# Denominators straight behind the product with V in all twelve key tiles, row-maximum pieces at three places a tile, and zero rows written between the x tiles

## The chip, the cores and the metric

The kernel runs on one core of one Trainium2 chip. The metric is the device time of one execution of the whole kernel in microseconds (us), the median of three runs. Its engines are TensorE (PE in the rows: matmuls; PEld: its weight loads), VectorE (DVE), ScalarE (ACT), GpSimd (POOL) and SyncE (SP, which here only issues transfers). Each works through its own list of instructions in order; they wait for each other by semaphores.

## The reference, cut to what matters

Four layers work on x of 2 x 1024 x 1024: attention, a mixing layer, a second attention and a layer with a small mixture of experts. Only the two attentions are touched. Both have 32 query heads, 8 key heads and a head size of 32, so that four query heads share one key head:

```python
q = (x @ wq).reshape(bsz, seq_len, N_HEADS, HEAD_DIM)
k = (x @ wk).reshape(bsz, seq_len, N_KV_HEADS, HEAD_DIM)
v = (x @ wv).reshape(bsz, seq_len, N_KV_HEADS, HEAD_DIM)
...
scores = jnp.einsum('bqhd,bkhd->bhqk', q, k) / np.float32(np.sqrt(HEAD_DIM))
scores = scores + mask
attn = jax.nn.softmax(scores.astype(jnp.float32), axis=-1).astype(q.dtype)
out = jnp.einsum('bhqk,bkhd->bqhd', attn, v).reshape(bsz, seq_len, N_HEADS * HEAD_DIM)
return out @ wo
```

## The kernel before, in words

**Groups.** `attention` is called once for each of the two attentions. For each of the two batches it runs a prologue (projections, first row maxima) and then eight groups, one per key head with its four query heads. Groups 0 to 5 of a batch follow the order `body`, group 6 `body6` (without a projection), group 7 `body7`, or `ahead7` in the first batch, which also prepares the next batch's x. That makes 24 groups of `body`, 4 of `body6`, 2 of `body7` and 2 of `ahead7` in the kernel.

**Tiles and steps.** A group has twelve key tiles (units 0 to 11): pairs of 512 queries and 128 keys on or below the diagonal. The list that `iteration` returns sets the order of every engine's work in the group. Its steps are:

- `("ST", e, half)`: scores of unit e, transposed, for two of the four heads (two matmuls into `pst`, line 827). ScalarE takes the exponential into `prob` (line 560), GpSimd masks a unit on the diagonal (line 464).
- `("PV", e, 0)`: the product of `prob` with V (`vg`) into `ppv`, below called V e. `("PV", e, 1)`: the product of the same `prob` with a matrix of ones into `pden`, the softmax denominators, below D e. Each is four products of 32 output rows, line 847, shown as x8 in the trace.
- `("S", k)`: piece k of the row maxima of the next group, k from 0 to 37. TensorE writes untransposed scores of one to four heads, at most 512 columns, into one of the two banks of `psh` (line 780). VectorE takes the maximum: line 650 for a piece below the diagonal, line 647 with its read of the accumulator for a piece on the diagonal, once per head.
- `("P", c, i)`: an eighth of a projection of 512 columns, three matmuls of line 759, also into `psh`. `MT`, `NORM`, `HI`, `LO`, `WS`, `RS` and others are steps of the other engines, or short.

**The two banks.** `bank_plan` gives pieces and projections the banks 0 and 1 of `psh` in turn. A piece may start when VectorE has freed its bank, that is when it has read the piece two before:

```python
pe.wait_ge(s["sh_free"], SH0 + u + prev + 1)
```

This wait stands ahead of the piece's weight load. Everything behind it in TensorE's list waits too.

**Where the pieces stand.** `iteration` spreads the 38 pieces over all steps of units 1 to 9 (`window`), in proportion to the columns that each step streams. `after[step]` holds what follows a step.

**The start of an attention.** For eight x tiles VectorE takes statistics and normalises (line 619), GpSimd computes 1/deviation (line 420), and TensorE transposes. GpSimd then writes the constant rows of `kst` and `qst` (lines 492, 494, 496), turns the first projection (`turn_over`, lines 432 and 434), and splits the second chunk of weights (`w_lo`, line 425), for which TensorE's second chunk of projections waits. The semaphore `padded` tells TensorE that the constant rows stand; it is read ahead of the first piece.

Of the kernel before, what the change touches and what calls it, by code (L numbers as in the profile page):

```python
# [14 lines left out]
F32 = mybir.dt.float32  # L15
# [6 lines left out]
P = 128  # L22
# [3 lines left out]
ST_ = S // P  # L26
# [3 lines left out]
GH = 4  # L30
# [46 lines left out]
def columns(step):  # L77

    what, e, _ = step
    n = BANK - unit_offset(e)  # L80
    return 2 * max(n, BANK // 2) if what == "ST" else 4 * n


def iteration(full_s=True, proj=True, ahead=False):

    steps = [[("ST", e + 1, 0), ("ST", e + 1, 1), ("PV", e, 0), ("PV", e, 1)] for e in range(NU)]
    steps[-1] = steps[-1][2:]  # L90
    after = {step: [] for unit in steps for step in unit}
    first = []
    if proj:
        quarter = lambda c, i: [("P", c, k) for k in range(i * PIECES // 4, (i + 1) * PIECES // 4)]
        first = quarter(0, 0)
        for i, step in enumerate(steps[0][:3]):
            after[step] += quarter(0, i + 1)
        after[steps[2][1]] += [("HI", 0)]
        after[steps[3][1]] += [("LO", 0)]
        after[steps[2][0]] += [("WL", 0)]  # L100
        after[steps[4][0]] += [("WS", 0)]
        after[steps[5][0]] += [("RS", 0)]
        after[steps[10][1]] += quarter(1, 0)
        after[steps[10][2]] += quarter(1, 1) + [("RK", 0)]
        after[steps[10][3]] += quarter(1, 2) + quarter(1, 3)
    if full_s:
        window = [step for unit in steps[1:10] for step in unit]
        total, done, k = sum(map(columns, window)), 0, 0
        for step in window:
            done += columns(step)  # L110
            while k < len(USES) and k * total < done * len(USES) - total // 2:
                after[step] += [("S", k)]
                k += 1
        assert k == len(USES)
        after[steps[10][1]] += [("MT", 0)]
    after[steps[10][1]] += [("NORM", 0)]
    if ahead:


        for i in range(ST_):  # L120
            after[steps[i][0]] += [("XS", i)]
            after[steps[i][2]] += [("XN", i)]
            after[steps[i + 2][1]] += [("XT", i)]
            after[steps[i + 2][2]] += [("XC", i)] + [("XL", i + NX_AHEAD)] * (i + NX_AHEAD < ST_)
        first = [("XL", i) for i in range(NX_AHEAD)]
        for i in range(PIECES):
            after[steps[10][i * 3 // PIECES]] += [("P", "next", i)]
    order = [("ST", 0, 0), ("ST", 0, 1)] + ([("HI", 1), ("LO", 1), ("RS", 1)] if full_s else []) + first
    for unit in steps:
        for step in unit:  # L130
            order += [step] + after[step]
    return order + [("NORM", 1)]


# [55 lines left out]
def attention(nc, sem, layer, x_in, wqkv, cos_in, sin_in, swap, oT_d):  # L190
# [21 lines left out]
    ZT0, W0, SH0, R0, E0, PV0, AC0, N0, ST0, DMA0 = 4, 2, 1, 4, 2, 2, 2, 1, 2, 16  # L212

    pro, body, body6, body7 = prologue(), iteration(), iteration(proj=False), iteration(False, False)
    ahead7 = iteration(False, False, True)
    plan_pro, U_PRO = bank_plan(pro, spare=(2, 3, 4, 5))
    plan = {id(order): bank_plan(order)[0] for order in (body, body6, body7, ahead7)}
# [4 lines left out]
    with ExitStack() as ctx:  # L222
        def sb(name, shape, dt=F32):
            return ctx.enter_context(nc.sbuf_tensor(f"a{layer}_{name}", shape, dt))
# [17 lines left out]
        qst = [sb(f"qst{i}", [P, GH, S], F32R) for i in range(2)]  # L242
# [173 lines left out]
        def _(pool):  # L416
            def reciprocal_deviation(tile, k):

                pool.wait_ge(s["stats"], tile + 1)
                pool.tensor_tensor(mv[k % 2][:, 3:4], mv[k % 2][:, 2:3], nhalf[:, :], ALU.pow).then_inc(s["pow"], 1)  # L420

            def w_lo(n, par):
                pool.wait_ge(s["w_hi"], n + 1)
                pool.sem_inc(s["pool_turn"], 1)
                pool.tensor_tensor(w[par][1][:, :, :], wraw[par][:, :, :], w[par][0][:, :, :].bitcast(F32),  # L425
                                   ALU.subtract).then_inc(s["w_ready"], 1)
# [56 lines left out]
            pool.drain().then_inc(s["const"], 1)  # L483
            pool.drain().then_inc(s["w_ready"], W0)
            pool.drain().then_inc(s["roped"], R0)
            for k in range(ST_):
                reciprocal_deviation(k, k)
                if k == 5:
                    w_lo(0, 0)
            pool.drain()  # L490
            for i in range(2):
                pool.memset(kst[i][96:P, :].bitcast(F32), -1.0)
                pool.drain()
                pool.memset(kst[i][96:P - 1, :].bitcast(F32), 0.0)
                pool.drain()
                pool.memset(qst[i][96:P - 1, :, :].bitcast(F32), 0.0)
                pool.drain()
            pool.drain().then_inc(s["padded"], 1)

# [248 lines left out]
        def _(pe):  # L748
            def project(n, u, where, par, c, piece):

                _, at, prev = where
                if piece == 0:
                    pe.wait_ge(s["w_ready"], W0 + n + 1)
                    pe.wait_ge(s["sh_free"], SH0 + u + prev + 1)
                passes = [(k, a, x) for k in range(KC) for a, x in ((0, 0), (0, 1), (1, 0))]
                step = len(passes) // PIECES
                for i in range(piece * step, (piece + 1) * step):
                    k, a, x = passes[i]
                    mm = pe.matmul(bank(at), w[par][a][:, k, :], xT[x][:, k, c * BANK:(c + 1) * BANK],  # L759
                                   start=(i == 0), stop=(i == len(passes) - 1))  # L760
                if piece == PIECES - 1:
                    mm.then_inc(s["sh_ready"], 1)
# [12 lines left out]
            def row_scores(u, where, par, k):  # L775
                _, at, prev = where
                qt, kc, n, heads, _ = USES[k]
                pe.wait_ge(s["sh_free"], SH0 + u + prev + 1)
                for i, h in enumerate(heads):
                    mm = pe.matmul(psh[:, at, i * n:(i + 1) * n], qst[par][0:P - 1, h, qt * P:(qt + 1) * P],  # L780
                                   kst[par][0:P - 1, kc * BANK:kc * BANK + n], start=True, stop=True,
                                   skip_group_check=True)
                mm.then_inc(s["sh_ready"], 1)

            def transpose_max(n, u, where):
                _, at, prev = where
                pe.wait_ge(s["mx_ready"], n + 1)
                pe.wait_ge(s["sh_free"], SH0 + u + prev + 1)
                pe.transpose(psh[0:GH * ST_, at, 0:P], mx[:, 0, :], ident[:, :]).then_inc(s["sh_ready"], 1)
# [1131 lines left out]
```

## Time and profile before

| | before |
|---|---|
| median of three runs | 3116.89 us (3111.95 to 3116.89) |
| the profiled execution's own time | 3121.41 us |
| its span, from the first to the last instruction | 3119.7 us |
| mean granted TensorE clock over the span | 0.945 |
| TensorE busy (matmuls) | 2780.3 us, 89% |
| VectorE busy | 1933.4 us, 62% |
| ScalarE busy | 1001.4 us, 32% |
| GpSimd busy | 715.2 us, 23% |

The span is the time that the rows below divide up. The profiled execution's own time is 1.7 us longer, and lies 4.5 us above the median of the three runs. A share of busy time is an average over all layers. What one stage waits for is read from that stage's rows.

### The profile page before, as it was taken

Reading aid. Unit: us, or ns where it says so; the run is one execution under the profiler, and the core shown is the slowest. Engines: PE = TensorE matmul, PEld = TensorE weight load, DVE = VectorE, ACT = ScalarE, POOL = GpSimd, SP = SyncE. Lnnn points to the kernel's source line nnn. Section 1 sums busy time; section 2 is a strip of 40 time slices with the busy share of each in tenths; the row PEclk is TensorE's granted clock in tenths of the full one; section 3 lists DMA queues with packets and bytes.
Section 4 is the critical chain, followed back from the end, with each engine's and each line's share of the span. In section 5 each row is a group of like instructions: output and inputs, shape, how many; then the busy total and the mean of one; then the engine's idle time right before and its main releaser. Section 6 shows DMA issues by size and latency. Waiting matters only on the chain. (4 is left out here: it accounts for less than half of the span.)

```text
span 3119.7 us, 49191 instructions
## 1 busy us (share of the span) xinstructions
PE 2780.3 (89%) x15824; PEld 1788.4 (57%) x15824; DVE 1933.4 (62%) x4357; ACT 1001.4 (32%) x1549; POOL 715.2 (23%) x693
## 2 busy tenths in 40 slices
PE   7899998999999799652859999989999996997999
PEld 5545554655554488652646455436555542885887
DVE  4577777557777433588765677775677774324543
ACT  2143435134343411352521443433244344101000
POOL 6223231433231000000044323214223220001111
PEclk8999999999999899765979999989999998998999
DMA  3323222323131422000123323223323221443111
GB/s 139 102 64 89 70 72 72 113 73 97 56 102 30 140 81 67 0 0 0 81 115 105 101 63 89 69 64 110 94 63 97 58 77 73 158 135 148 68 67 41
DMA packets 121063, 252.84 MB, mean 81 GB/s; under 512 B 12720, under 2 KB 39728, under 8 KB 120880
## 3 DMA queue, kind: packets, MB, share of 16 engines
q1 hardware_dynamic: 120912, 251.03, 25.5%
q8 instruction: 69, 1.13, 0.2%
q14 instruction: 82, 0.67, 0.1%
HBM read 166.57 MB, written 84.41 MB: 80 GB/s over the span
## 5 line engine op out<-in xcount | busy, mean ns | idle before, releaser
L560 ACT ACTIVATE a_prob<-a_pst 128x1024 f32<-128x1024 f32 (+3 forms) x768 | 593.0, 814 | 726.2 <-PE a_pst L827 724.7
L647 DVE CUSTOM_DVE_ANT_0 a_psh<-a_psh,a_edge 128x128 f32<-128x128 f32 (+3 forms) x1024 | 487.6, 514 | 218.5 <-PE a_psh L780 208.1
L780 PE MATMUL a_psh<-a_kst,a_qst 127*128 127x512 f32 (+3 forms) x1536 | 511.7, 394 | 29.3 <-issue 12.0
L780 PEld LDWEIGHTS a_psh<-a_kst,a_qst 127*128 127x128 f32 x1536 | 255.9, 189 | 455.4 <-DVE a_mx L647 199.3
L827 PE MATMUL a_pst<-a_qst,a_kst 128*128 128x512 f32 (+2 forms) x1536 | 398.8, 361 | 28.9 <-ACT a_prob L560 11.0
L650 DVE TENSOR_REDUCE a_mx<-a_psh 128x1 f32<-128x512 f32 x512 | 343.6, 689 | 71.1 <-PE a_psh L780 65.1
L847 PE MATMUL a_ppv<-a_prob,a_vg 128*32 128x512 f32 (+3 forms) x3072 | 335.0, 508 | 15.6 <-POOL a_prob L464 10.6
L464 POOL TENSOR_SCALAR_AFFINE_SELECT a_prob<-a_prob 128x512 f32<-128x512 f32 x256 | 171.9, 672 | 759.4 <-ACT a_prob L560 758.2
L827 PEld LDWEIGHTS a_pst<-a_qst,a_kst 128*128 128x128 f32 x1536 | 267.1, 192 | 128.4 <-issue 56.2
L847 PE MATMUL a_pden<-a_prob,a_ones 128*32 128x512 f32 (+3 forms) x3072 | 332.0, 504 | 0.0
L691 DVE RECIPROCAL a_dens<-a_dens 128x512 f32<-128x512 f32 x64 | 214.6, 3353 | 75.6 <-ACT a_dens L568 66.4
L432 POOL TENSOR_TENSOR a_swp<-a_swp,a_sin 128x512 f32<-128x512 f32 x80 | 103.2, 1290 | 330.3 <-DVE a_swp L636 329.6
L759 PE MATMUL a_psh<-a_xT_hi,a_w_hi 128*128 128x512 f32 x416 | 174.4, 419 | 2.3 <-issue 1.6
L1411 PE MATMUL h_pout<-h_w,h_o 128*128 128x512 f32 x720 | 167.7, 392 | 0.8 <-DVE h_x L1288 0.8
L759 PE MATMUL a_psh<-a_xT_lo,a_w_hi 128*128 128x512 f32 x416 | 165.2, 397 | 0.0
L759 PE MATMUL a_psh<-a_xT_hi,a_w_lo 128*128 128x512 f32 x416 | 164.9, 396 | 0.0
L425 POOL TENSOR_TENSOR a_w_lo<-a_wraw,a_w_hi 128x1024 fp32r<-128x1024 f32 x50 | 119.2, 2383 | 178.9 <-ACT a_w_hi L536 163.0
L759 PE MATMUL a_pst<-a_xT_hi,a_w_hi 128*128 128x512 f32 x352 | 141.7, 403 | 13.2 <-POOL a_w_lo L425 9.0
L1411 PEld LDWEIGHTS h_pout<-h_w,h_o 128*128 128x128 f32 x720 | 134.1, 188 | 28.8 <-DMA h_wb<-in_w_branch 1.2
L647 DVE DVE_READ_ACCUMULATOR2_ANT a_mx<- 128x1 f32 x1024 | 145.0, 142 | 0.0
L759 PE MATMUL a_pst<-a_xT_lo,a_w_hi 128*128 128x512 f32 x352 | 139.5, 396 | 0.0
L759 PE MATMUL a_pst<-a_xT_hi,a_w_lo 128*128 128x512 f32 x352 | 139.1, 395 | 0.0
(217 smaller groups left out, 3958.8 us busy)
## 6 DMA issues: line engine op xcount, KB each, us to landing
a_qst<-q SPq DMA_DIRECT2D x192, 256.0 KB, 4.5
a_wraw<-in_wqkv SPq DMA_DIRECT2D x52, 512.0 KB, 5.7
q<-a_stg_hi SPq DMA_DIRECT2D x64, 256.0 KB, 2.6
q<-a_stg_lo SPq DMA_DIRECT2D x64, 256.0 KB, 2.8
oT<-a_oT SPq DMA_DIRECT2D x64, 256.0 KB, 2.5
a_kst<-kT SPq DMA_DIRECT2D x96, 128.0 KB, 3.0
h_oraw<-oT SPq DMA_DIRECT2D x16, 512.0 KB, 4.1
h_x<-in_x SPq DMA_DIRECT2D x16, 512.0 KB, 4.7
```

The source lines that it names most:

```text
L425: pool.tensor_tensor(w[par][1][:, :, :], wraw[par][:, :, :], w[par][0][:, :, :].bitcast(F32), ALU.subtract).then_inc(s["w_ready"], 1)
L432: pool.tensor_tensor(swp[c][:, :], swp[c][:, :], sin[:, c * BANK:(c + 1) * BANK], ALU.mult)
L464: pool.affine_select(out=blk, in_=blk, compare_op=ALU.is_ge, fill=0.0, base=0, pattern=[[0, GH], [1, P]], channel_multiplier=-1)\
L560: act.activation(prob[k % 2][:, 2 * half:2 * half + 2, off:], pst[:, half, :, off:], ACT.Exp, scale=scale).then_inc(s["exp_done"], 1)
L647: part = dve.tensor_tensor_reduce(scores, scores, edge[:, BANK - n:], 1.0, 2 * MASKED, ALU.add, ALU.max, mx_hq[kc][:, h, qt:qt + 1])
L650: part = dve.tensor_reduce(mx_hq[kc][:, heads[0]:heads[0] + m, qt], psh[:, at, 0:m * n].rearrange("p (m n) -> p m n", n=n), AX.X, ALU.max)
L691: dve.reciprocal(dens[:, :], dens[:, :])
L759: mm = pe.matmul(bank(at), w[par][a][:, k, :], xT[x][:, k, c * BANK:(c + 1) * BANK], start=(i == 0), stop=(i == len(passes) - 1))
L780: mm = pe.matmul(psh[:, at, i * n:(i + 1) * n], qst[par][0:P - 1, h, qt * P:(qt + 1) * P], kst[par][0:P - 1, kc * BANK:kc * BANK + n], sta ...
L827: mm = pe.matmul(pst[:, half, hh, off:], kst[par][:, ki * P:(ki + 1) * P], qst[par][:, 2 * half + hh, qc * BANK + off:(qc + 1) * BANK], st ...
L847: mm = pe.matmul(acc[h * HD:(h + 1) * HD, off:], lhs, prob[k % 2][:, h, off:], start=(ki == 0), stop=(ki == 4 * qc + 3), skip_group_check= ...
L1411: mm = pe.matmul(pout[:, half, :], o[:, par, a, k, :], w[:, b, k, half * BANK:(half + 1) * BANK], start=(i == 0), stop=(i == len(passes) - 1))
```

## The change

`open_slots` keeps the two ST steps and D of each unit as places behind which pieces are put, and takes out V. What stood behind V is now put behind D, ahead of what stood there already. So D follows V directly in all twelve units, and the pieces have three places a unit: behind each of the two ST steps and behind D. At the start of each attention the constant rows of `kst` are written first, and the zero rows of `qst` in eight parts (one head of one of the two buffers), each behind the 1/deviation of one x tile.

```diff
+def open_slots(units):
+
+    return [step for unit in units for step in unit if step[0] != "PV" or step[2] == 1]
...
     if full_s:
-        window = [step for unit in steps[1:10] for step in unit]
+        window = open_slots(steps[1:10])
...
     for unit in steps:
         for step in unit:
-            order += [step] + after[step]
+            if step[0] == "PV" and step[2] == 0:
+                order += [step]
+            elif step[0] == "PV":
+                order += [step] + after["PV", step[1], 0] + after[step]
+            else:
+                order += [step] + after[step]
...
-            for k in range(ST_):
-                reciprocal_deviation(k, k)
-                if k == 5:
-                    w_lo(0, 0)
-            pool.drain()
             for i in range(2):
                 pool.memset(kst[i][96:P, :].bitcast(F32), -1.0)
                 pool.drain()
                 pool.memset(kst[i][96:P - 1, :].bitcast(F32), 0.0)
                 pool.drain()
-                pool.memset(qst[i][96:P - 1, :, :].bitcast(F32), 0.0)
+            for k in range(ST_):
+                reciprocal_deviation(k, k)
+                if k == 5:
+                    w_lo(0, 0)
+                pool.drain()
+                pool.memset(qst[k // GH][96:P - 1, k % GH, :].bitcast(F32), 0.0)
                 pool.drain()
             pool.drain().then_inc(s["padded"], 1)
```

The first place is TensorE's list in `body`, around the products of unit 5. Before, from the second ST of unit 6 (which stands ahead of V 5) to piece 18; `a_pst` is ST, `a_ppv` is V, `a_pden` is D, `a_psh` with `a_kst` is a piece:

```order
L827 MATMUL a_pst<-a_qst,a_kst 128x512 x2
L778 REGISTER_ALU
L780 MATMUL a_psh<-a_kst,a_qst 128x128 x4
L841 REGISTER_ALU
L847 MATMUL a_ppv<-a_prob,a_vg 32x512 x4
L778 REGISTER_ALU
L780 MATMUL a_psh<-a_kst,a_qst 128x512
L847 MATMUL a_pden<-a_prob,a_ones 32x512 x4
L778 REGISTER_ALU
L780 MATMUL a_psh<-a_kst,a_qst 128x512
L778 REGISTER_ALU
L780 MATMUL a_psh<-a_kst,a_qst 128x512
```

And now, at the same place (line numbers are ten higher):

```order
L837 MATMUL a_pst<-a_qst,a_kst 128x512 x2
L788 REGISTER_ALU
L790 MATMUL a_psh<-a_kst,a_qst 128x512
L851 REGISTER_ALU
L857 MATMUL a_ppv<-a_prob,a_vg 32x512 x4
L857 MATMUL a_pden<-a_prob,a_ones 32x512 x4
L788 REGISTER_ALU
L790 MATMUL a_psh<-a_kst,a_qst 128x512
L788 REGISTER_ALU
L790 MATMUL a_psh<-a_kst,a_qst 128x512
L788 REGISTER_ALU
L790 MATMUL a_psh<-a_kst,a_qst 128x512
```

Piece 16, which parted V 5 from D 5, now stands ahead of V 5, and three pieces (17, 18, 19) instead of two stand behind D 5 before the next ST.

The second place is GpSimd's list at the start of an attention, from the end of its constants to the first `turn_over`. Before (`a_mv` is the 1/deviation of an x tile, `a_swp` the first instruction of `turn_over`):

```order
L420 TENSOR_TENSOR a_mv<-a_mv,a_nhalf 128x1 x6
L425 TENSOR_TENSOR a_w_lo<-a_wraw,a_w_hi 128x1024
L420 TENSOR_TENSOR a_mv<-a_mv,a_nhalf 128x1 x2
L492 MEMSET a_kst 32x1024
L494 MEMSET a_kst 31x1024
L496 MEMSET a_qst 31x4096
L492 MEMSET a_kst 32x1024
L494 MEMSET a_kst 31x1024
L496 MEMSET a_qst 31x4096
L432 TENSOR_TENSOR a_swp<-a_swp,a_sin 128x512
```

And now its last part, from the sixth x tile on (the four `a_kst` rows and five pairs like the first two rows stand ahead):

```order
L430 TENSOR_TENSOR a_mv<-a_mv,a_nhalf 128x1
L435 TENSOR_TENSOR a_w_lo<-a_wraw,a_w_hi 128x1024
L506 MEMSET a_qst 31x1024
L430 TENSOR_TENSOR a_mv<-a_mv,a_nhalf 128x1
L506 MEMSET a_qst 31x1024
L430 TENSOR_TENSOR a_mv<-a_mv,a_nhalf 128x1
L506 MEMSET a_qst 31x1024
L442 TENSOR_TENSOR a_swp<-a_swp,a_sin 128x512
```

Only one short memset is left between the last 1/deviation and `turn_over`. VectorE's, ScalarE's, SyncE's and GpSimd's order in the groups stays as it was, but for `ahead7`, where ScalarE copies the accumulators of unit 3 ahead of an x tile. The bank of every piece stays the same too.

## Rows read from the trace of the kernel before

**Rows 1.** The page: granted TensorE clock in 40 slices, tenths of full speed.

```profile
PEclk8999999999999899765979999989999998998999
```

**Rows 2.** Four `body` groups: busy time by engine; longest waits among weight loads.

```profile
242.40:454.29 211.89, 211.40 (x1349) 111.37 (x1349) 157.89 (x369) 88.81 (x124) 63.05 (x64) 1.00 0.27 78
...
PEld a_psh L780 <- DVE a_mx L647: 24.4, 40, 0.8
...
PEld a_psh L780 <- DVE a_mx L650: 21.1, 32, 0.8
```

**Rows 3.** Timeline of PE: start, us, engine, line, operation; first rows of two groups.

```profile
911.15 1.21 PE L827 MATMUL a_pst<-a_qst,a_kst 128*128 128x512 f32 x4
...
964.14 1.21 PE L827 MATMUL a_pst<-a_qst,a_kst 128*128 128x512 f32 x4
```

**Rows 4.** Timeline of PE in `body`: piece 16 to piece 20.

```profile
936.54 0.51 PE L780 MATMUL a_psh<-a_kst,a_qst 127*128 127x512 f32 x1
936.98 1.06 PE L847 MATMUL a_pden<-a_prob,a_ones 128*32 128x512 f32 x8
937.97 0.73 PE L780 MATMUL a_psh<-a_kst,a_qst 127*128 127x512 f32 x2
938.54 0.64 PE L827 MATMUL a_pst<-a_qst,a_kst 128*128 128x512 f32 x2
939.26 0.50 PE L780 MATMUL a_psh<-a_kst,a_qst 127*128 127x512 f32 x1
939.59 0.63 PE L827 MATMUL a_pst<-a_qst,a_kst 128*128 128x512 f32 x2
940.07 0.40 PE L780 MATMUL a_psh<-a_kst,a_qst 127*128 127x256 f32 x2
```

**Rows 5.** Timeline of DVE: maxima of piece 8 and of pieces 17 to 19.

```profile
929.41 0.70 DVE L647 CUSTOM_DVE_ANT_0 a_psh<-a_psh,a_edge 128x512 f32<-128x512 f32 x1 [0.25 <-PE a_psh L780]
930.02 0.14 DVE L647 DVE_READ_ACCUMULATOR2_ANT a_mx<- 128x1 f32 x1
...
938.51 1.98 DVE L650 TENSOR_REDUCE a_mx<-a_psh 128x1 f32<-128x512 f32 x3 [0.73 <-PE a_psh L780]
```

**Rows 6.** Timeline of PE in `body7`, where nothing parts V and D.

```profile
1034.22 1.06 PE L847 MATMUL a_ppv<-a_prob,a_vg 128*32 128x512 f32 x8
1035.10 1.04 PE L847 MATMUL a_pden<-a_prob,a_ones 128*32 128x512 f32 x8
1036.07 1.20 PE L827 MATMUL a_pst<-a_qst,a_kst 128*128 128x512 f32 x4
```

**Rows 7.** Timeline of POOL at the start of the first attention.

```profile
29.64 0.95 POOL L492 MEMSET a_kst<- 32x1024 f32 x1
...
41.81 1.28 POOL L432 TENSOR_TENSOR a_swp<-a_swp,a_sin 128x512 f32<-128x512 f32 x1 [0.37 <-issue]
...
44.46 2.34 POOL L425 TENSOR_TENSOR a_w_lo<-a_wraw,a_w_hi 128x1024 fp32r<-128x1024 f32 x1
```

**Rows 8.** Timeline of DVE at the start of the first attention.

```profile
24.66 0.81 DVE L619 TENSOR_SCALAR a_prob<-a_prob,a_mv 128x1024 f32<-128x1024 f32 x1
...
30.56 1.65 DVE L619 TENSOR_SCALAR a_xin<-a_xin,a_mv 128x1024 f32<-128x1024 f32 x1
...
36.23 0.72 DVE L711 STREAM_SHUFFLE a_swp<-a_psh 128x512 f32<-128x512 f32 x1
```

**Rows 9.** Timeline of PE at the start of both attentions.

```profile
46.85 0.80 PE L759 MATMUL a_pst<-a_xT_hi,a_w_hi 128*128 128x512 f32 x1 [4.06 <-POOL a_w_lo L425]
...
50.37 0.40 PE L759 MATMUL a_pst<-a_xT_hi,a_w_lo 128*128 128x512 f32 x1
50.60 0.39 PE L759 MATMUL a_pst<-a_xT_hi,a_w_hi 128*128 128x512 f32 x1
...
1632.51 0.80 PE L759 MATMUL a_pst<-a_xT_hi,a_w_hi 128*128 128x512 f32 x1 [4.92 <-POOL a_w_lo L425]
...
1637.37 0.46 PE L759 MATMUL a_pst<-a_xT_hi,a_w_lo 128*128 128x512 f32 x1
```

## The prediction, made before the changed kernel ran

> **What bounds the kernel now.** I read the page first: TensorE's busy share is the highest of the engines (the table above), and the granted clock stands near full speed in most slices [rows 1]. The share over the whole kernel says little, so I went on to the stage that the change touches. In four `body` groups (211.89 us) TensorE is busy for 211.40 us and the clock is granted in full [rows 2]. So a `body` group is bound by TensorE's list: whatever its matmuls take, or wait for, is the time. One group lasts 964.14 - 911.15 = 53.0 us [rows 3].
>
> The same view has a warning. TensorE's weight loads for the pieces wait for VectorE in 40 + 32 = 72 of the 4 x 38 = 152 pieces, 45.5 us in all [rows 2]. These waits cost almost nothing today because the matmuls ahead of the piece are still streaming. They show that the two banks are handed back only just in time.
>
> **What the edit of the order saves.** The change lets D follow V without a piece between. I read the price of parting them from the timeline of TensorE. D 5 takes 937.97 - 936.98 = 0.99 us until the next matmul, which is a piece [rows 4]; V followed by D takes 1035.10 - 1034.22 = 0.88 us [rows 6]. Leaving a product for another kind of matmul costs 0.11 us. The single 512-column piece between V and D takes 936.98 - 936.54 = 0.44 us [rows 4], where the same matmul among its like takes 0.23 us (50.60 - 50.37 in a projection [rows 9]; two ST matmuls of 512 columns take 940.07 - 939.59 = 0.48 us [rows 4]). So 0.21 us go to being first behind a product and last ahead of one. Together a split costs 0.32 us; I take 0.31, since some splits hold smaller pieces.
>
> In `body` V and D are parted in ten units (0, 1, 2, 4 to 10), in `body6` in eight (1, 2, 4 to 9), in `ahead7` in one, in `body7` in none. That is 3.1, 2.5, 0.3 and 0 us a group.
>
> **What it adds.** All pieces now stand at three places, and V and D together are a block of about 1.9 us (0.88 + 0.99) in which VectorE can have at most the two pieces that the two banks hold. Behind the block come up to three pieces in a row. The third needs the bank of the first.
>
> The turnaround of a bank is in the rows. Pieces 17 and 18 start at 937.97; VectorE starts on 17 at 938.51, 0.54 later; three maxima in a row take 1.98 us, which is 0.69 for one and 0.645 for each further; piece 19, in the bank of 17, starts at 939.26, so 1.29 us behind 17 [rows 4, 5]. It followed an ST step that began at 938.54 and needed 0.46, so it was some 0.26 us late, and its slot was 939.59 - 939.26 = 0.33 us, not 0.23: a late piece also shows its weight load.
>
> Now put three 512-column pieces directly behind D. The third could start at 0.34 + 0.23 = 0.57 us and gets its bank at 1.29: 0.72 us of wait. That is the case for pieces 17, 18, 19; for 22, 23, 24; and for 32, 33, 34. A maximum on the diagonal is slower: its read of the accumulator comes 0.61 us after its start and takes 0.14, and the bank is free only then [rows 5].
>
> I walked through a whole `body` group in this way, TensorE's list against VectorE's: a matmul of 512 columns 0.23, 384 0.18, 256 0.12 and 128 0.10 us, a product by 4/2400 us a column, the 0.11 and 0.2 us of each change of kind, 0.54 us from a piece to its maximum where VectorE is free, 0.645 us for a maximum below the diagonal, 0.06 from a free bank to the piece. For the order of before the walk gives 53.1 us a group against the 53.0 measured, with 0.6 us of waits for banks (at piece 19 above all, as in [rows 4]). For the new order it gives these waits: piece 3 0.84, piece 4 0.25, 8 0.37, 11 0.50, 14 0.27, 15 0.31, 19 0.73, 24 0.73, 27 0.32, 30 0.53, 34 0.73, and 0.49 at the projection step behind piece 37. The sum is 6.1 us, 5.5 more than before. Eleven late starts instead of six show their weight load, 0.1 us each: 0.5 more. Against that stand the 3.1 us of the splits. Net +2.9 us for `body`.
>
> `body6` has the same pieces and eight splits: 6.0 - 2.5 = +3.5; I take 3.4, since its last wait overlaps with one that it has for the row maxima. `ahead7` gains 0.3. The sum is 24 x 2.9 + 4 x 3.4 - 2 x 0.3 = 69.6 + 13.6 - 0.6 = **+82.6 us**.
>
> What is queued behind the waiting piece is the next ST or V. ScalarE and GpSimd get their scores later, but they idle between units today; the next group's row maxima come later by what the group grows and are still needed only at its end. They add nothing.
>
> **The zero rows.** At the start of an attention TensorE waits 4.06 us for `w_lo`, from 42.79 on; in the second attention 4.92 us [rows 9]. `w_lo` ran at 44.46, behind `turn_over` at 41.81, behind six memsets from 29.64 to 0.37 us before `turn_over` [rows 7]. VectorE had the projection ready at 36.95 [rows 8]. Without the memsets `turn_over` starts at 37.05, takes 2.65, `w_lo` 2.34: ready at 42.04, ahead of TensorE. The wait goes. The idle time had a second price: behind it TensorE runs at half clock, eight matmuls in 50.37 - 46.85 = 3.52 us where 0.23 each make 1.8, and in the second attention eleven in 4.86 where they need 2.5 [rows 9]. So 4.06 + 1.7 + 4.92 + 2.3 = 13.0 us are gained.
>
> The memsets now lie where VectorE works, and there is one price. A normalisation takes 0.81 us, and 1.65 with a memset on GpSimd at its side [rows 7, 8]: it waited. Today one of eight does. In the new order the four `kst` memsets (1.07 each) end near 7 us, when the first 1/deviation is due, and the first `qst` part may catch the first normalisation; later a part ends over 1 us before the next. So one is paid and one saved, about zero; if none is saved, 2 x 0.85 = 1.7 are lost. If the clock would have dropped anyway, only 9.0 are gained. Bounds -7 to -13; I take **-13**.
>
> **Sum.** +82.6 - 13.0 = +69.6 us on the profiled execution, 3121.4 to 3191. That execution lay 4.5 us over the median, which gives **3187 us**.
>
> **Unknown costs.** The walk rests on hand-over times. With the hand-over 0.07 us shorter, banks handed back at once, or maxima of 0.60 us, a `body` group gains 2.6 to 2.8 us. If a late piece hides its weight load, 2.4. If the 0.1 us for the first matmul behind a product is not saved by joining, 3.6. I widen to 2.0 and 3.7: 28 groups make +56 to +104, with the zero rows +43 to +97.
>
> **The rivals.**
>
> 1. *The banks keep up, and the splits' price is simply saved* (faster). V and D joined save 24 x 3.1 + 4 x 2.5 + 0.6 = 85 us, and the zero rows 13: 3117 - 98 = 3019 us. For it speaks that VectorE is idle for a quarter of a group (157.89 of 211.89 busy [rows 2]). Against it, the 1.29 us turnaround is seen in the rows and lies against 0.57 us of work. It decides if the waits grow by less than 3.1 us a group; my walk says 6.0. Chance 0.06.
>
> 2. *The waits grow by about what the joins save* (near zero or slightly faster). With some 3 us a group only the 13 us are left, and 3104 us follow; with 3.6 us, no change. Its mechanism is VectorE starting on a piece earlier than its row shows. Chance 0.06.
>
> 3. *The clock falls too* (slower still). TensorE would sit idle twelve times a group. At the start of the attentions it ran at half clock after an idle stretch, and lost 1.7 us in each fall that short [rows 9]. One such fall in each of 28 groups adds 48 us: 3235 us. Against it, the four groups show full clock [rows 2] and no single new wait is over 0.9 us. The Trainium skill, TensorE: Matmul & The Clock Gate, section on the second failure mode (cycling through PSUM banks), says that short idles between groups of matmuls, forced by the queue of banks, can swing the clock; it speaks against this change, and the trace so far shows such a fall only behind idle times of over 4 us. Chance 0.08.
>
> My forecast has 0.80.
>
> **Range and chances.** The forecast's own range of +43 to +97 is 3160 to 3214. To hold 8 in 10 I let it reach part of the way to the clock case above and to smaller waits below: 3150 to 3222. From here 0.2% is 6 us, about what a measurement of this kernel can tell from no change. Faster by more: rival 1 and most of 2, 0.10. Within: 0.02. Slower: 0.88.
>
> **What the profile of the changed kernel would show.** Right: a `body` group of 55.9 us, V and D of 512 columns 0.88 us apart, the third piece behind D 1.3 us behind the first, TensorE's idle time before line 790 by VectorE at some 6 us a group; no wait for `w_lo` at the start of the attentions and full clock there; normalisations of 0.81 us but for at most one. Wrong: groups of 50 us (rival 1), or below 1.0 granted clock in the groups (rival 3). I would be wrong too if the walk misses a coupling that the old order never used, such as ScalarE's exponential coming too late for V.

## The result, and the profile after

The changed kernel takes 3182.86 us (median of 4 runs, 3178.94 to 3187.77) against 3116.89 us (median of 4 runs, 3111.95 to 3120.95): a ratio of 1.0212, 95% interval 1.0199 to 1.0225, so 66 us slower. The forecast was 3187 us. The profiled execution took 3178.94 us with a span of 3177.2 us; its span is 57.5 us longer than that of before. Its mean clock is 0.949.

The page of the changed kernel: span, busy times, the granted clock in 40 slices, and from its list of costliest groups the pieces (busy time, mean ns of one, and behind the bar the idle time of TensorE just before them):

```profile
span 3177.2 us, 49229 instructions
PE 2741.3 (86%) x15824; PEld 1813.0 (57%) x15824; DVE 1912.5 (60%) x4357; ACT 1009.9 (32%) x1549; POOL 714.0 (22%) x705
PEclk9999999999999899866979999999999999998999
L790 PE MATMUL a_psh<-a_kst,a_qst 127*128 127x512 f32 (+3 forms) x1536 | 511.3, 389 | 121.0 <-DVE a_mx L660 46.3
```

TensorE is busy for 39 us less (89% to 86% of the span) and the kernel is longer: work was saved and waiting put in its place. 121.0 us of idle time stand directly before pieces; before the change they were 29.3 us.

Four `body` groups of the changed kernel by windows (span of the stretch, then busy time of PE, PEld, DVE, ACT and POOL, clock, DMA share, GB/s), and what TensorE's matmuls waited for in them (total us, times, longest us):

```profile
1853.06:2074.89 221.83, 206.66 (x1352) 115.75 (x1348) 154.39 (x369) 90.09 (x124) 62.95 (x64) 1.00 0.27 74
...
PE a_psh L790 <- DVE a_mx L660: 6.6, 12, 0.6
PE a_psh L790 <- DVE a_mx L657: 5.2, 12, 0.6
PE a_psh L769 <- DVE a_mx L657: 1.1, 4, 0.3
```

Before, TensorE was busy for 211.40 of 211.89 us here [rows 2]. Now it is for 206.66 of 221.83: a group has 15.17 / 4 = 3.8 us of idle time. The clock stays at 1.00, and VectorE has not more to do than before; it has only its work at other times. A whole group by its first rows (as [rows 3]), and the place of [rows 4], where three pieces stand behind a product:

```profile
936.87 1.21 PE L837 MATMUL a_pst<-a_qst,a_kst 128*128 128x512 f32 x4
...
963.01 1.07 PE L857 MATMUL a_ppv<-a_prob,a_vg 128*32 128x512 f32 x8
963.89 1.04 PE L857 MATMUL a_pden<-a_prob,a_ones 128*32 128x512 f32 x8
964.86 0.73 PE L790 MATMUL a_psh<-a_kst,a_qst 127*128 127x512 f32 x2
966.15 0.50 PE L790 MATMUL a_psh<-a_kst,a_qst 127*128 127x512 f32 x1 [0.55 <-DVE a_mx L660]
966.48 0.62 PE L837 MATMUL a_pst<-a_qst,a_kst 128*128 128x512 f32 x2
...
992.47 1.21 PE L837 MATMUL a_pst<-a_qst,a_kst 128*128 128x512 f32 x4
```

One group takes 992.47 - 936.87 = 55.60 us; over the 20 `body` groups that are not the first of a batch the mean is 55.49, against 53.02 (in the four groups of the windows 55.46 against 52.97). V to D is 963.89 - 963.01 = 0.88 us, as in [rows 6], and D to the next matmul 0.97. The third piece behind D starts 966.15 - 964.86 = 1.29 us behind the first and takes 966.48 - 966.15 = 0.33 us. VectorE's timeline shows the other side of that wait:

```profile
965.40 1.98 DVE L660 TENSOR_REDUCE a_mx<-a_psh 128x1 f32<-128x512 f32 x3 [1.23 <-PE a_psh L790]
```

VectorE had waited 1.23 us for this piece, since no piece comes during V and D. It starts 0.54 us behind the piece (965.40 - 964.86), and needs 0.69 us for the maximum; then the bank is free. TensorE and VectorE now wait for each other in turn.

The start of the first attention after the change: GpSimd, VectorE and TensorE.

```profile
7.73 0.95 POOL L506 MEMSET a_qst<- 31x1024 f32 x1
...
25.39 0.95 POOL L506 MEMSET a_qst<- 31x1024 f32 x1
...
37.60 1.30 POOL L442 TENSOR_TENSOR a_swp<-a_swp,a_sin 128x512 f32<-128x512 f32 x1 [5.60 <-DVE a_swp L721]
...
40.29 2.40 POOL L435 TENSOR_TENSOR a_w_lo<-a_wraw,a_w_hi 128x1024 fp32r<-128x1024 f32 x1
```

```profile
7.73 1.50 DVE L629 TENSOR_SCALAR a_xin<-a_xin,a_mv 128x1024 f32<-128x1024 f32 x1
...
25.34 1.55 DVE L629 TENSOR_SCALAR a_prob<-a_prob,a_mv 128x1024 f32<-128x1024 f32 x1
...
31.62 0.93 DVE L629 TENSOR_SCALAR a_xin<-a_xin,a_mv 128x1024 f32<-128x1024 f32 x1
...
36.71 0.72 DVE L721 STREAM_SHUFFLE a_swp<-a_psh 128x512 f32<-128x512 f32 x1
```

```profile
42.66 0.39 PE L769 MATMUL a_pst<-a_xT_lo,a_w_hi 128*128 128x512 f32 x1
42.89 0.39 PE L769 MATMUL a_pst<-a_xT_hi,a_w_lo 128*128 128x512 f32 x1
43.12 0.39 PE L769 MATMUL a_pst<-a_xT_hi,a_w_hi 128*128 128x512 f32 x1
```

`turn_over` starts at 37.60 instead of 41.81 [rows 7], `w_lo` is ready at 42.69, and TensorE's second chunk follows with 0.23 us a matmul and no wait, where [rows 9] had 4.06 us of wait and half clock behind it. The first memset and the first normalisation run side by side at 7.73, and the normalisation takes 1.50 us for 0.81. The same happens once more, at the sixth x tile: there the memset stands behind a `w_lo`, starts at 25.39, and the normalisation beside it takes 1.55 us. The last one, which took 1.65 [rows 8], takes 0.93. So two are stretched, where before it was one.

### The profile page after: what moved, and what is told of

Read it like the earlier page. It is cut to its first block and busy times, and to the rows that moved or that the text cites. A ratio compares the mean times of both kernels' runs of the same rounds, so it can differ in the third digit from the quotient of the medians.

```text
span 3177.2 us, 49229 instructions
## 1 busy us (share of the span) xinstructions
PE 2741.3 (86%) x15824; PEld 1813.0 (57%) x15824; DVE 1912.5 (60%) x4357; ACT 1009.9 (32%) x1549; POOL 714.0 (22%) x705
## 5 line engine op out<-in xcount | busy, mean ns | idle before, releaser
L790 PE MATMUL a_psh<-a_kst,a_qst 127*128 127x512 f32 (+3 forms) x1536 | 511.3, 389 | 121.0 <-DVE a_mx L660 46.3
L837 PE MATMUL a_pst<-a_qst,a_kst 128*128 128x512 f32 (+2 forms) x1536 | 411.8, 363 | 28.1 <-DMA a_qst<-rowmax 10.2
L857 PE MATMUL a_pden<-a_prob,a_ones 128*32 128x512 f32 (+3 forms) x3072 | 323.5, 493 | 0.0
L857 PEld LDWEIGHTS a_pden<-a_prob,a_ones 128*32 128x32 f32 x3072 | 100.3, 112 | 155.7 <-issue 144.9
```

Of the source, the lines that this page charges most:

```text
L837: mm = pe.matmul(pst[:, half, hh, off:], kst[par][:, ki * P:(ki + 1) * P], qst[par][:, 2 * half + hh, qc * BANK + off:(qc + 1) * BANK], st ...
L857: mm = pe.matmul(acc[h * HD:(h + 1) * HD, off:], lhs, prob[k % 2][:, h, off:], start=(ki == 0), stop=(ki == 4 * qc + 3), skip_group_check= ...
```

## The experiments

The kernel before ran beside the experiments, on the chip that they ran on. Its median was 3116.94 us beside the first four, and 3114.59 us beside the last four. Ratios are against it. The `body` group of a table is the mean of four or more groups of the run's trace.

### The two parts apart

`e1_zero_rows_only` is the kernel before with only the new place of the memsets. `e2_order_only` is the changed kernel with the memsets where they were.

> The kernel before with only the zero rows moved between the x tiles. Theory A (the wait for w_lo and the half clock behind it go): TensorE starts its second chunk of projections without a wait in both attentions, and the kernel gains 4.7 us before the first group and some 7 us in the second attention, 12 us in all, about 3105 us beside 3117. Rival B (a memset at the side of a normalisation delays the x tiles and eats the gain): under 6 us. Rival C (the gain is given back at the first pieces, which wait for their keys and queries by DMA): the first group starts earlier but its third unit no earlier, under 3 us in all.

> The changed kernel with the zero rows written as before, so the new order alone. Theory A (two parts that add up): a body group of 55.5 us as in the changed kernel, 53.0 before, and 66 + 12 = 78 us over the kernel before, about 3195 us. Rival (part of the slowdown came from the earlier start, such as the first group's longer waits for its keys and queries): 66 us over the kernel before or less, about 3183 us.

| | median us | runs | ratio (95% interval) | span | `body` group |
|---|---|---|---|---|---|
| `e1_zero_rows_only` | 3104.54 | 7 | 0.9961 (0.9947 to 0.9975) | 3101.7 | 52.9 to 53.0 |
| `e2_order_only` | 3195.96 | 4 | 1.0253 (1.0233 to 1.0273) | 3190.9 | 55.45 |

The memsets alone give -12.4 us (3104.54 - 3116.94), the order alone +79.0. Together they make +66.6, and both at once were measured at +66.0. So the two parts add up within 1 us, and the slower kernel hides a gain of 0.4%.

### V and D joined in one unit alone

Here the kernel before keeps its order, but for one unit of the 24 `body` groups: in `e3_join_10` D follows V directly in unit 10, in `e4_join_0` in unit 0. What stood behind V goes behind D.

```diff
+JOINED = (10,)
...
-            order += [step] + after[step]
+            if step[0] == "PV" and step[1] in JOINED and full_s and proj:
+                order += [step] + (after["PV", step[1], 0] + after[step] if step[2] else [])
+            else:
+                order += [step] + after[step]
```

> The kernel before, with D straight behind V in unit 10 of body alone; projection steps, no row-maximum pieces, stood between. Theory A (a split costs 0.31 us where no bank is short): 24 x 0.31 = 7.4 us faster, about 3109 us, a body group of 52.7 us. Rival (the price of a split is no price of TensorE's time, because what follows waits for the banks anyway): no change, 3117 us.

> The same edit in unit 0 of body alone, where the last two steps of the first projection stood between. Theory A (bound by the two banks): the projection now ends just ahead of piece 0, VectorE turns it (1.35 us) when the first pieces want their banks, and piece 1 or 3 waits; my walk through the two lists gives 53.8 us a body group, 0.9 us more, so about 20 us slower, 3138 us. Rival B (only the split counts): 7.4 us faster, 3109 us.

| | median us | runs | ratio (95% interval) | span | `body` group |
|---|---|---|---|---|---|
| `e3_join_10` | 3111.49 | 10 | 0.9978 (0.9965 to 0.9990) | 3112.5 | 52.6 |
| `e4_join_0` | 3133.29 | 7 | 1.0049 (1.0035 to 1.0062) | 3131.2 | 53.7 |

Joining is worth what the rows said when nothing else goes wrong: 0.38 us a group in the trace, and 5.45 / 24 = 0.23 us by the medians (0.13 to 0.45 by the interval), around the predicted 0.31.

In unit 0 the same edit costs 0.7 us a group. I had expected that size (0.9), but from a wait for a bank. The trace names another. In the waits of TensorE in four groups, and in its timeline, V 2 waits for GpSimd's mask:

```profile
1832.00:2046.71 214.71, 210.27 (x1348) 112.07 (x1348) 156.92 (x369) 89.03 (x124) 62.86 (x64) 1.00 0.27 76
...
PE a_ppv L851 <- POOL a_prob L468: 3.9, 4, 1.0
...
1846.43 0.64 PE L851 MATMUL a_ppv<-a_prob,a_vg 128*32 128x256 f32 x8 [0.97 <-POOL a_prob L468]
```

GpSimd's timeline shows why the mask is late:

```profile
1843.09 1.27 POOL L436 TENSOR_TENSOR a_swp<-a_swp,a_sin 128x512 f32<-128x512 f32 x1 [4.13 <-DVE a_swp L640]
1844.51 1.28 POOL L438 TENSOR_TENSOR a_rot<-a_rot,a_swp 128x512 f32<-128x512 f32 x1
1845.74 1.23 POOL L468 TENSOR_SCALAR_AFFINE_SELECT a_prob<-a_prob 128x512 f32<-128x512 f32 x2
```

The projection steps that stood between V 0 and D 0 now end later, so `turn_over` starts later, and the mask of unit 2 is behind it in GpSimd's list. So this run showed nothing of the banks. It showed a second price that my prediction did not have: a delayed projection can reach V through GpSimd. In the changed kernel no wait of V for the mask is among the waits of four groups above. What hides it there can be read from `e6_short_maxima_new`, two experiments below, which has the same order: the wait at piece 3 shrinks from 0.64 to 0.37 us, and V 2 waits 0.34 us for the mask instead. From the first ST of unit 3 to V 2 TensorE takes 2.05 us there, against 2.18 in the changed kernel.

```profile
1798.09 0.64 PE L857 MATMUL a_ppv<-a_prob,a_vg 128*32 128x256 f32 x8 [0.34 <-POOL a_prob L474]
```

So in the changed kernel TensorE reaches V 2 late already, by its waits at pieces 3 and 4, and nearly all of these two waits would be taken over by the mask if the banks came back sooner.

### The third pieces put elsewhere

`e5_third_piece_later` is the changed kernel with pieces 19, 24 and 34, the third ones directly behind a D of 512 columns, each moved behind the next ST. All other pieces stay. `PLACES` gives for each piece its step among those of units 1 to 9.

```diff
+PLACES = [0, 3, 3, 4, 5, 7, 8, 9, 9, 12, 13, 13, 15, 15, 16, 16, 17, 19, 19, 20, 20, 21, 23, 23, 24, 24, 25, 25, 27, 27, 28, 29, 31, 31, 32, 33, 35, 35]
...
-        window = open_slots(steps[1:10])
...
+        window = [step for unit in steps[1:10] for step in unit]
+        for k, place in enumerate(PLACES):
+            after[window[place]] += [("S", k)]
```

> The changed kernel with pieces 19, 24 and 34, each the third behind D, moved behind the first ST step of the next unit. Theory A (VectorE has only two pieces to work on during V and D, so the time lost is VectorE's, and a piece moved back by one ST waits there instead): a body group of 55.4 us, 0.1 us less, some 3 us in all, about 3180 us. Rival B (as my prediction worded it: the third piece behind D holds TensorE up by 0.72 us, and without three in a row the wait is gone): 28 x 3 x 0.72 = 60 us faster than the changed kernel, about 3123 us.

It took 3175.05 us (4 runs), ratio 1.0199 (1.0180 to 1.0218). That is 60.5 us over the kernel before beside it, where the changed kernel lay 66.0 over; the two intervals overlap, so the medians alone hardly tell them apart. A group takes 55.12 us instead of 55.46 in the traces. Windows and waits of four groups, then the timeline of TensorE at a unit where the wait now comes later:

```profile
1849.37:2069.86 220.49, 209.34 (x1353) 116.19 (x1349) 153.72 (x369) 91.47 (x124) 63.05 (x64) 1.00 0.27 74
...
PE a_psh L786 <- DVE a_mx L653: 5.4, 14, 0.6
PE a_psh L786 <- DVE a_mx L656: 1.2, 4, 0.3
...
1887.48 0.62 PE L786 MATMUL a_psh<-a_kst,a_qst 127*128 127x384 f32 x2
1888.79 0.50 PE L786 MATMUL a_psh<-a_kst,a_qst 127*128 127x512 f32 x1 [0.33 <-DVE a_mx L653]
```

The three waits of 0.72 us did go, but most of their time was lost again further on: against the changed kernel, unit 5 is 1.05 us shorter and unit 6 0.10, unit 7 is 0.97 longer, unit 8 1.07 shorter, unit 9 0.92 longer (each moved piece takes its own slot along). Of 3 x 0.72 = 2.2 us only 0.33 us a group are gained. So a late third piece was where the wait showed, not what made it. At the V and D of unit 5 VectorE stood idle for 1.23 us, before the change for 0.73 [rows 5], and the pieces that it didn't take then are due in the next units. A place that relieves one piece loads the next.

### VectorE's maxima made short

If VectorE's pace through two banks is what TensorE waits for, shorter maxima must give the time back, and must give far less to the kernel before. Both kernels take each maximum over only the first 128 columns of a head's scores, so that the maxima of larger pieces are incomplete, and on the diagonal take the mask's last 128 columns for them. All matmuls, places and banks stay.

```diff
-                        scores = psh[:, at, i * n:(i + 1) * n]
+                        scores = psh[:, at, i * n:i * n + P]
...
-                                             psh[:, at, 0:m * n].rearrange("p (m n) -> p m n", n=n), AX.X, ALU.max)
+                                             psh[:, at, 0:m * P].rearrange("p (m n) -> p m n", n=P), AX.X, ALU.max)
```

> The changed kernel with maxima over the first 128 columns of each head's scores alone; the rest of the columns is left out of the maximum. VectorE frees a bank in some 0.25 us a head, not up to 0.65. Theory A (bank and VectorE hold the time): the waits between the pieces go, and a body group falls from 55.5 to 51.9 us; 1.7 us of waits are left, at the first pieces, which wait for VectorE to turn the projection. About 28 x 3.5 = 98 us faster than the changed kernel, 3085 us. Rival (TensorE is slowed by the new order itself): no change, 3183 us.

> The kernel before with the same short maxima; the same columns are left out. Theory A: a body group falls from 53.0 to 52.0 us only, about 28 us, 3089 us. Rival (shorter maxima help by as much in either order, since VectorE is what is short): 98 us faster as in the new order, 3019 us.

| | median us | runs | ratio (95% interval) | `body` group |
|---|---|---|---|---|
| `e6_short_maxima_new` (changed kernel) | 3058.4 | 2 | 0.9823 (0.9799 to 0.9847) | 51.7 |
| `e7_short_maxima_old` (kernel before) | 3060.63 | 2 | 0.9830 (0.9807 to 0.9853) | 51.73 |

Four groups of each, `e6_short_maxima_new` first with its waits:

```profile
1783.73:1990.50 206.77, 201.78 (x1348) 115.93 (x1348) 106.08 (x369) 90.09 (x124) 62.89 (x64) 1.00 0.28 79
...
PE a_psh L790 <- DVE a_mx L657: 1.5, 4, 0.4
PE a_ppv L857 <- POOL a_prob L474: 1.4, 4, 0.3
PE a_psh L790 <- DVE a_mx L660: 0.9, 6, 0.2
```

```profile
1784.23:1991.15 206.92, 206.92 (x1353) 111.65 (x1349) 106.64 (x369) 88.33 (x124) 62.95 (x64) 1.00 0.28 79
```

In the new order a group gets 3.8 us shorter and the waits for banks shrink from 12.9 to 2.4 us in four groups: VectorE's pace is what the new order waits for. Both rivals fell: the new order was not slow by itself, and the order of before gained 1.24 us a group, a third as much. That is still more than the 0.6 us of waits that the walk gave it. So [rows 2], with 211.40 of 211.89 us busy, hid over 1 us a group: a late piece shows its weight load and a longer slot, which is counted as busy.

Both medians are some 27 us lower than expected (3085 and 3089 us), because the whole kernels gain more than their groups give. Against the kernel before beside each, the new order went from +66.0 to -56.2 us, of which 28 x 3.8 = 106 are the groups', and the old order gained 54 us, of which 28 x 1.24 = 35 are. The other 16 to 19 us fit the prologues, whose maxima were cut too: ahead of the first group alone the traces show 124.63 - 119.69 = 4.9 us in the new order and 129.33 - 124.34 = 5.0 in the old, and there are four prologues.

With short maxima both orders meet at 51.7 us, although the new one has none of the ten splits. TensorE is still idle there for 5.0 us in four groups (206.77 - 201.78).

### New places, with the gaps where they cost nothing

The last kernel uses what came before: V and D joined in unit 10, where that paid; the zero rows between the x tiles; and pieces at places searched with the walk of the prediction. The places are put in as in `e5_third_piece_later`, and the join as in `e3_join_10`. In units 2 and 5 they leave no piece between V and D, so these two are joined as well: V and D are parted in seven units, not in nine.

```diff
...
+JOINED = (10,)
+PLACES = [0, 0, 2, 3, 4, 7, 8, 9, 11, 12, 13, 14, 14, 15, 15, 17, 17, 19, 19, 21, 21, 22, 22, 23, 24, 25, 26, 26, 27, 27, 29, 30, 30, 31, 31, 34, 34, 35]
...
```

> A version built from the findings: V and D stay parted as before, except in unit 10; the 38 pieces stand at places found by walking through the two lists, so that VectorE always has a piece and its banks are free in time; zero rows as in the change. Theory A: a body group of 51.5 us, 1.4 less than before, body6 1.0 less, 12 us from the zero rows: 51 us faster than the kernel before, about 3066 us. Rival (the places of before were good enough, the walk's tenths are not real): only the zero rows and unit 10, 18 us, 3099 us.

It took 3078.0 us (5 runs), ratio 0.9883 (0.9864 to 0.9902): 36.6 us less than the kernel before, of which some 12.4 are the zero rows, and over 100 less than the changed kernel. Expected were 51 us less, by the rival 18. The windows of four groups, and V 5 with D 5:

```profile
1791.23:1998.55 207.32, 206.98 (x1353) 112.92 (x1349) 156.85 (x369) 88.77 (x124) 63.08 (x64) 1.00 0.28 79
...
1814.68 0.89 PE L780 MATMUL a_psh<-a_kst,a_qst 127*128 127x128 f32 x5
1815.50 1.06 PE L847 MATMUL a_ppv<-a_prob,a_vg 128*32 128x512 f32 x8
1816.38 1.04 PE L847 MATMUL a_pden<-a_prob,a_ones 128*32 128x512 f32 x8
1817.36 0.74 PE L780 MATMUL a_psh<-a_kst,a_qst 127*128 127x512 f32 x2
```

A group takes 207.32 / 4 = 51.83 us, with VectorE doing all its work (156.85 us); expected were 51.5. That is 1.14 us less than before. It would be wrong to put all of it down to the banks. Three joins (units 2, 5 and 10) at the 0.23 to 0.38 us of `e3_join_10` are 0.7 to 1.1 us of it by themselves, as an estimate, so at most some 0.4 us come from banks that are free sooner. Nor does the short-maxima kernel of the old order (51.73, with ten splits) show that nothing is left: by the same estimate it would lie 0.7 to 1.1 us lower with seven splits. And the weight loads of pieces wait for VectorE 72 times in these four groups, 46.9 us, as often as before (72 times, 45.5 us [rows 2]). A matmul's wait is in the list of neither kernel, so its absence says nothing.

What the rows do show is that a join need not cost a wait. Around unit 5, pieces 15 and 16 fill both banks right ahead of V, only pieces 17 and 18 stand behind D, and none of them waits; in the changed kernel a third piece followed and waited. How much of the gain is due to each place was not measured one by one.

## Why the prediction was right

**The body group** was the term that decided. Predicted 53.0 to 55.9 us (+2.9), measured 55.49 for 53.02 (+2.48) in 20 of the 24 groups. Its parts:

- *The joins, -3.1.* The step held: V to D 0.88 us, and `e3_join_10` gave 0.23 to 0.38 us a split for the 0.31.
- *The waits, 0.6 to 6.1 us.* The page shows idle gaps, and the end of a matmul is modelled some 0.16 us behind its last hand-over, so a wait of 0.72 stands there as 0.55. With 0.16 added to each of the twelve gaps the sum is 5.7 us: 0.80 for piece 3, 0.24 for 4, 0.31 for 8, 0.48 for 11, 0.25 and 0.26 for 14 and 15, 0.72 for 19, 0.71 for 24, 0.31 for 27, 0.49 for 30, 0.71 for 34, 0.44 at the projection step. The walk had named these twelve places, each within 0.05 us but for piece 8 (0.37 predicted). That the sum is 0.4 lower is nearly the whole difference.
- *That VectorE's pace sets them* was tested by `e6_short_maxima_new` and `e7_short_maxima_old`: right. That the third piece behind D holds TensorE up is true of where the wait shows. As a price of that place it would have been wrong, as `e5_third_piece_later` shows (0.33 of over 2 us was gained).
- *What it had wrong.* The weight loads' waits in the order of before "cost almost nothing": `e7_short_maxima_old` got 1.24 us a group back. And ScalarE and GpSimd "add nothing": the mask would hold V 2 if the waits at pieces 3 and 4 did not come first (0.34 us in `e6_short_maxima_new`). Neither changed the sum, the second only because of those waits.

The four first groups of a batch went another way: -1.92, +6.15, +1.32 and +4.80 us. Ahead of piece 0 they also wait for the stacked keys and queries that a transfer brings (0.38 to 4.66 us before, 0.83 to 3.56 after), and the granted clock falls in most: the group with +6.15 had 1.00 before and 0.92 after. That they come to 10.35, near four times 2.9, is chance. All 24 together make 20 x 2.48 + 10.35 = +59.9 us for the +69.6 predicted.

**body6** was predicted at +3.4 each and measured at +2.57, +1.63, +2.13 and +1.64: 8.0 us for 13.6. Most of the difference lies in the profiled execution of before, not in the order. In three of its four `body6` groups TensorE ran V 0 and D 0 wholly or in part at half clock, behind a wait of 0.99 us for transposed V; in the other one piece 11 waited 0.78 us for a transfer. The timeline of TensorE before and after, and the windows around V 0 and D 0 in the first two of the four groups before (the granted clock stands third from the end; in the other two it is 0.50 and 0.54):

```profile
968.93 1.94 PE L847 MATMUL a_ppv<-a_prob,a_vg 128*32 128x512 f32 x8 [0.99 <-POOL a_vg L446]
970.61 1.68 PE L847 MATMUL a_pden<-a_prob,a_ones 128*32 128x512 f32 x8
972.23 0.74 PE L827 MATMUL a_pst<-a_qst,a_kst 128*128 128x256 f32 x4
```

```profile
997.25 1.07 PE L857 MATMUL a_ppv<-a_prob,a_vg 128*32 128x512 f32 x8 [0.98 <-POOL a_vg L456]
998.11 1.07 PE L857 MATMUL a_pden<-a_prob,a_ones 128*32 128x512 f32 x8
999.10 0.50 PE L837 MATMUL a_pst<-a_qst,a_kst 128*128 128x256 f32 x2
```

```profile
459.00:462.00 3.00, 2.92 (x24) 1.50 (x24) 1.75 (x1) 1.64 (x3) 2.17 (x2) 1.00 0.06 23
969.00:972.00 3.00, 3.00 (x16) 0.58 (x16) 1.63 (x1) 1.02 (x2) 2.01 (x2) 0.52 0.11 41
```

972.23 - 968.93 = 3.30 us before, 1.85 after, with the same wait ahead (0.99 and 0.98); after, no group fell. The order doesn't decide this: `e1_zero_rows_only`, with the groups of before, had such a fall in two of four, and `e2_order_only`, with those of the changed kernel, in one (that group took 52.17 us, its others 50.51 to 50.85). Where neither a fall nor that transfer came in between, `body6` took 47.42 to 47.84 us in the order of before (in `e1_zero_rows_only`, `e3_join_10` and `e4_join_0`, which leave it as it was) and 50.68 to 50.85 in the changed kernel: about 3.2 more, so the predicted 3.4 was nearly right. Why the clock falls in some of these groups and not in others is open.

**The last groups** (`ahead7`) were predicted at -0.3 each; group 7 of a batch with the prologue behind it was +1.45 in the first and +0.93 in the second attention. What made them longer is open.

**The zero rows** were predicted at -13.0, measured at -4.7 us ahead of the first group (124.63 for 129.33) and -7.3 from the last group of the first attention to the first of the second: -12.0, and -12.4 by the medians of `e1_zero_rows_only`. The wait is gone and the clock behind it is full. The price was read too low: two normalisations are stretched in the first attention (1.50 and 1.55 us) for the one of before, and two in the second (1.34 and 1.54) for none, since `w_lo` pushes the sixth memset onto the next one. Of the 1.1 us missing there some 0.5 are a later start: the first projection is ready at 36.71 instead of 36.23 [rows 8]. The rest is no more than two executions of the same instructions differ by: `e2_order_only`, whose start is that of before, began its first group at 128.03.

**The sum** is 59.9 + 8.0 + 2.4 - 12.0 = +58.3 us for the span, which grew by 57.5; the rest, -0.8, lies behind the last `body6`. The medians moved by 66.0. The profiled execution of before lay 4.5 us over its median and that of after 3.9 under its own, which is the 8.4 us between the two. So the forecast of 3187 was closer (4 us) than its terms (a predicted +69.6 against +58.3 of the span), and that closeness is in part luck.

**The rivals.** Rival 1 (banks keep up) needed waits that grow by less than 3.1 us a group, and rival 2 by about 3; they are 5.7 for 0.6. Rival 3 (the clock falls too) did not come about in the 20 groups: 12 idle times a group, 15.17 of 221.83 us in four, and the granted clock is 1.00. The Trainium skill, TensorE: Matmul & The Clock Gate, section on the second failure mode, warns of short idles forced by the queue of banks; at this size (0.6 us at most) no such fall is seen in these groups. But the prediction's own argument against rival 3, that the trace shows a fall only behind idle times of over 4 us, was a misreading: the trace of before has the three falls in `body6`, each behind a wait of 0.99 us.

## What to carry to other kernels

A step that parts two long products costs its switches (0.3 us here), but it is also the moment at which the consumer gets work. Before joining, compare how long the consumer can work on what the banks hold with the length of the joined block: here VectorE stood idle for 1.23 us at a block of 1.85 us, and a third piece behind it waited 0.72. Two full banks ahead of the block and only two pieces behind it went without a wait. A gap seen at one piece is a debt of the whole stretch: moving three such pieces gained 0.33 of 2.2 us, while new places for all of them, with seven of the ten splits kept, gave back all that the change had lost and 1.14 us a group more, of which 0.7 to 1.1 are the price of the three splits. Time the parts of a mixed change apart: here 12.4 us of gain lay beneath 79.0 us of loss. And before a difference between two traces is put down to the order, look at the granted clock of the same stretch in other runs.

## What the runs showed of the hardware

- **Busy is not unhindered.** With TensorE at 211.40 busy of 211.89 us, 1.24 us a group still came back when VectorE's maxima were shortened.
- **The clock and idle times.** Twelve idles of 0.1 to 0.6 us a group left the granted clock at 1.00. A wait of 0.99 us with V and D behind it went with half clock in three of four groups in the trace of before, in two of four in `e1_zero_rows_only`, in one in `e2_order_only` and in none after the change. A wait of 4.06 us at an attention's start cost 1.7 us more at half clock [rows 9], and `e1_zero_rows_only` got both back.
- **A memset slows VectorE.** One of 0.95 us on GpSimd, which only writes, stretched a normalisation beside it from 0.81 to 1.50 us, and another to 1.55.
- **GpSimd's order reaches TensorE.** With the projection steps of unit 0 behind D 0, a mask behind `turn_over` made V 2 wait 0.97 us.
